# Layer 0's mixture of experts: the whole up product of the shared expert ahead of the first slot group

## The reference, cut to what matters

```
def _swiglu(x, wg, wu, wd):
    return jax.nn.silu(x @ wg) * (x @ wu) @ wd
logits = xn @ gate_w.T                      # xn: layernorm(x) * scale + bias
tk_probs, tk_idx = jax.lax.top_k(softmax(logits), 2)
w = ...                                     # the two weights of a token, made to sum to one
out = _swiglu(xf, sWg, sWu, sWd)            # the shared expert, all 512 tokens
for e in range(8):
    out = out + w[:, e:e + 1] * _swiglu(xf, Wg[e], Wu[e], Wd[e])
x = x + out
```

## Time and profile before

| | us |
|---|---|
| median of 3 runs | 3748.93 |
| lowest and highest run | 3747.81, 3753.61 |
| the profiled execution | 3748.13 |
| its span | 3746.2 |
| TensorE busy in the span | 3193.1 (85%) |
| mean DMA rate over the span | 175 GB/s |
| stage of the change | about 461 to 893 of the span |

### The profile page before, as it was taken

The page is one execution under the profiler, slowest core; times in us unless marked ns, Lnnn a source line. Parts: engine busy times, 40 slices in busy tenths (PEclk is TensorE's granted clock), DMA queues, the critical chain, the costliest instruction groups (busy, mean ns, idle before and its releaser), DMA issues. The chain is left out here.

```text
span 3746.2 us, 41895 instructions
## 1 busy us (share of the span) xinstructions
PE 3193.1 (85%) x16921; PEld 1560.7 (42%) x16921; DVE 1201.4 (32%) x2501; ACT 700.4 (19%) x1281; POOL 115.7 (3%) x148
## 2 busy tenths in 40 slices
PE   8998789985899799889688987798998897666666
PEld 4444443432444444344356564434444573111111
DVE  3555420002344579735232132212444411000000
ACT  2442101011233231100012120112343121000000
POOL 1000010001000000000000000000000100000000
PEclk9999889997899899979899999899998999787778
DMA  3100079995111212121440120692001236999998
GB/s 138 40 31 35 34 325 414 425 422 204 56 45 45 70 34 72 52 90 45 173 165 23 53 92 12 287 400 111 32 25 44 106 135 282 420 420 420 420 420 367
DMA packets 102709, 654.05 MB, mean 175 GB/s; under 512 B 18850, under 2 KB 28066, under 8 KB 39586
## 3 DMA queue, kind: packets, MB, share of 16 engines
q1 hardware_dynamic: 98402, 638.31, 42.2%
q0 software_dynamic: 4160, 13.63, 1.0%
HBM read 642.40 MB, written 9.50 MB: 174 GB/s over the span
## 5 line engine op out<-in xcount | busy, mean ns | idle before, releaser
L770 PE MATMUL banks<-wvb,ctxT 128*128 128x512 f32 x512 | 230.9, 596 | 0.0
L2654 PE MATMUL banks<-ring,h 128*32 128x512 f32 x1024 | 172.0, 791 | 65.6 <-DMA ring<-in_L_ffn_w 41.4
L2642 PE MATMUL banks<-ring,mine 128*32 128x512 f32 x1024 | 163.9, 703 | 71.3 <-DMA ring<-in_L_ffn_w 69.9
L1631 PE MATMUL banks<-ring,xT 128*64 128x512 f32 x736 | 165.5, 603 | 14.6 <-DMA ring<-in_L_ffn_Wu 6.8
L494 PE MATMUL banks<-normed_features,ctxT 128*128 128x256 f32 x768 | 168.0, 379 | 1.1 <-ACT normed_features L460 1.1
L494 PEld LDWEIGHTS banks<-normed_features,ctxT 128*128 128x128 f32 x768 | 144.6, 190 | 23.0 <-issue 3.2
L2743 DVE COPY mine<-mT 128x32 f32<-128x32 f32 x31 | 5.6, 181 | 449.6 <-PE banks L2642 449.6
L770 PEld LDWEIGHTS banks<-wvb,ctxT 128*128 128x128 f32 x512 | 92.8, 190 | 108.6 <-issue 106.2
L766 PE MATMUL banks<-extraT,wkb 128*128 128x512 f32 x256 | 116.9, 611 | 1.0 <-ACT extraT L876 1.0
L766 PE MATMUL banks<-ring 128*128 128x512 f32 x256 | 115.4, 595 | 1.4 <-PEq L141 1.4
L766 PE MATMUL banks<-ctxT,wkb 128*128 128x512 f32 x256 | 115.4, 595 | 1.4 <-PEq L141 1.4
(11 more groups left out here) (570 smaller groups left out, 4684.0 us busy)
## 6 DMA issues: line engine op xcount, KB each, us to landing
ring<-in_L_ffn_w SPq DMA_DIRECT2D x256, 1024.0 KB, 26.8
ring<-in_L_ffn_Wd SPq DMA_DIRECT2D x24, 2048.0 KB, 23.5
ring<-in_L_ffn_Wg SPq DMA_DIRECT2D x23, 2048.0 KB, 18.3
ring<-in_L_ffn_Wu SPq DMA_DIRECT2D x23, 2048.0 KB, 20.9
wa<-in_L_ffn_W SPq DMA_DIRECT2D x32, 1024.0 KB, 12.6
wb<-in_L_ffn_W SPq DMA_DIRECT2D x32, 1024.0 KB, 10.4
ctxT<-in_ctxT SPq DMA_DIRECT2D x16, 1024.0 KB, 4.9
extra<-in_ctx SPq DMA_DIRECT2D x8, 1024.0 KB, 6.8
```

The costliest lines, as they stand in the source:

```text
L770: ins = pe.matmul(ps[:, u % 2, :], ctxT[:, par, k, r * P:(r + 1) * P], wvb[:, k, :], start=(k == 0), stop=(k == C - 1))
L1631: ins = pe.matmul(ps[H * side:H * side + H, 2 * kind + half, :], xT[:, p % 2, k, H * own:H * own + H], rows_of(where[(name, slot)], C)[:, ...
L2642: ins = pe.matmul(ps[B4 * q:B4 * q + B4, 0, :], mine[:, e % 2, k, :], w[:, q * 512:(q + 1) * 512], start=(k == 0), stop=(k == C - 1))
L2654: ins = pe.matmul(ps[B4 * q:B4 * q + B4, 2, :], h[:, Q * n + q, :], w[:, q * D:(q + 1) * D], start=(n == 0), stop=(n == Q - 1))
```

## The change

The list of units starts with both up units, and none stands behind group 2. On TensorE, ScalarE and VectorE parts 4 to 7 of the shared up product follow parts 0 to 3, ahead of group 0; group 0 waits for all eight. The place behind group 2 and the wait ahead of group 3 are gone. No operation is added or dropped.

```
-    UP_AFTER, DOWN_AFTER = 2, 6
+    DOWN_AFTER = 6
...
-    units.append(("up", 0))
-    read_by.append((up_done, 4))
+    for half in range(2):
+        units.append(("up", half))
+        read_by.append((up_done, 4 * half + 4))
...
-        if p == UP_AFTER:
-            units.append(("up", 1))
-            read_by.append((up_done, FC))
...
-                for n in range(4):
+                for n in range(FC):
                     shared_up(n)
                     if n == 1:
                         rank()
-                pe.wait_ge(*hs_ready.at(4))
+                pe.wait_ge(*hs_ready.at(FC))
                 turn_x(0)
...
-                            if p == UP_AFTER + 1:
-                                pe.wait_ge(*hs_ready.at(FC))
...
-                    if p == UP_AFTER:
-                        for n in range(4, FC):
-                            shared_up(n)
...
-                for n in range(4):
+                for n in range(FC):
                     shared_silu(n)
-                act.wait_ge(*hs_ready.at(4))
+                act.wait_ge(*hs_ready.at(FC))
                 take_x(0)
...
-                    if p == UP_AFTER:
-                        for n in range(4, FC):
-                            shared_silu(n)
...
-                shared_h(3)
+                for n in range(3, FC):
+                    shared_h(n)
...
-                    if p == UP_AFTER:
-                        for n in range(4, FC):
-                            shared_h(n)
```

## The result

The changed kernel takes 3763.75 us (median of 9 runs, 3753.32 to 3772.1) against 3749.9 us for the kernel before (9 runs, 3745.13 to 3761.33). The ratio is 1.0030 with a 95% interval of 1.0018 to 1.0041, so +11 us, between +7 and +15. The two medians lie 13.9 us apart; the ratio is taken from the single runs. The forecast was +12 and 3761. The change is slower, and by about what was said; the scatter of whole executions is too wide to tell +10 from +12.

The account below looks back on a forecast made before the run. The prediction took the start of the unbroken weight stream and the units behind it to bound the stage. Its terms, 17.4 - 4.9 - 0.7 = +11.8 us, gave a median of 3761 us, range 3753 to 3768.

Parts of the forecast that it names:

- stream theory: Expert stage: the weight stream's start, set by group 0's first gate product, and the units behind it set the end; 74%.
- Step 1 and 2: Front of the stage: group 0 starts 19.4 us later, 2.08 us of clock come back, stream starts +17.4 us.
- Step 3: Ahead of the stream: a second unit gets through on idle engines, leaving 62 units instead of 63 behind; -4.9 us.
- Step 4: Behind group 2: without the block of parts 4 to 7 the queue no longer runs thin; -0.7 us, between 0 and 1.7.
- Step 5: Shared down product: frees nothing for 27.73 us, but seven of eight places in flight, 34 us, keep the queue fed; 0.
- Step 6: Other engines' passes, third load of rows and SyncE's extra 0.6 us issue long before the gate: all at nothing.
- TensorE as the bound: Rival for the stage: TensorE's chain sets the end, so the change gains -11.9 us, a median of 3737; 6%.
- The clock at the waits: Rival: TensorE's clock falls at waits for landings; in the last group up to 13 us more, 3774; 12%.
- each time: Skill's claim that waiting for a transfer between bursts always throttles the array again; by it the full 13 us are paid.

Follow-up runs that it names:

- e1: Kernel before with 32 additional matmuls, results unused, between part 3 and the first slot group; ratio to the kernel before 1.0049 (1.0031 to 1.0068).
- e5: Kernel before with the ranks computed behind part 0 instead of part 1, so the scatter of rows starts sooner; ratio 0.9974 (0.9963 to 0.9985).
- e2: Changed kernel with parts 4 to 7 cut to one of four contraction steps; ratio to the kernel before 0.9974 (0.9961 to 0.9986).
- e4: Kernel before with parts 4 to 7, behind group 2, cut to one of four contraction steps, all transfers kept; ratio 0.9995 (0.9982 to 1.0008).
- e11: Changed kernel, unedited, timed and profiled a second time; ratio to the kernel before 1.0022 (1.0013 to 1.0030).
- e7: Changed kernel with five units sent ahead and the other three issued at the start of the expert block; ratio to the kernel before 1.0020 (1.0010 to 1.0031).
- e3: Kernel before without the transfer of unit up 1; parts 4 to 7 read slot 5's Wd instead; ratio 0.9992 (0.9980 to 1.0004).
- e6: Kernel before with the unit issued at 515 held until the first slot group's rows have landed; ratio 0.9981 (0.9972 to 0.9990).
- e9: Kernel before with early ranks and the block of parts 4 to 7 with its unit behind group 3; ratio 0.9956 (0.9944 to 0.9969).
- e8: Kernel before with 8 additional unused matmuls in TensorE's wait ahead of the first rows' turn; ratio 1.0007 (0.9998 to 1.0017).
- e10: Kernel before without unit up 1's transfer and with parts 4 to 7 cut to one of four contraction steps; ratio 0.9970 (0.9960 to 0.9981).
- e12: Changed kernel with the ranks computed behind part 0; ratio to the kernel before 1.0031 (1.0020 to 1.0041).

## Why the prediction was right

The mechanism was right: the start of the stream and the transfers behind it set the end of the stage. The sizes of two terms were off, by -2.0 and +0.9 us, and the two misses partly cancel. That the time came within 1 us of the forecast is in part luck, since it scatters by more.

**The view that decided it** was the windows with their DMA share beside TensorE's near 85%. The stream theory's three statements hold: a late start goes through in full (e1), an early one too (e5), and work in the middle is worth little (e2, e4).

**Step 1 and 2, the start of the stream.** Forecast +17.4; measured +17.06 (e11) and +17.02 (e7); +21.03 in the one profile with the slow clock in front. The four parts took 27.5 to 27.7 us, the wait behind them 1.41, the turn 1.40, the clock came back.

**Step 3, the unit.** Forecast -4.9. From the stream's start to the last Wd product the queue of the ring moved 132.12 MB in the kernel before and 130.03 in the changed one, 63.0 and 62.0 units. B fell by 6.7 and 6.8 in both profiles of the changed kernel. e3 shows that the -4.9 is no property of the unit: it holds only because the block left the middle too.

**Step 4, the block,** was mis-sized: -0.7 forecast, from one dip less another. Summed over windows of 4 us from 600 to 672 against 427 GB/s, the kernel before loses 2.8 us, the changed one 0.2 and 0.1. So about -2.7. The prediction took the dip at 750 to 756 as the price of the slots' rows and subtracted it; but e4, with these rows and a short block, loses 0.2 us in the middle, so the dip behind the block was nearly all empty queue.

**Step 5 failed, by 1 us.** The down block was to cost nothing, with seven of eight places in flight for its 27.73 us. Over 720 to 792 the kernel before loses 1.1 us, the changed one 2.1 and 1.9. SyncE's queue and what q1 had moved, first in the kernel before (535.46 to 716.37, and to 865.38), then in the changed one (560.76 to 734.68, and to 883.96):

```profile
716.37 26.91 SPq L1520 DMA_DIRECT2D ring<-in_L_ffn_Wg  x2
749.97 1.44 SPq L1520 DMA_DIRECT2D ring<-in_L_ffn_Wu  x2
q1 hardware_dynamic: 5843, 71.91, 95.1%
q1 hardware_dynamic: 9984, 132.12, 95.3%
...
734.68 26.91 SPq L1518 DMA_DIRECT2D ring<-in_L_ffn_Wg  x2
768.27 1.44 SPq L1518 DMA_DIRECT2D ring<-in_L_ffn_Wu  x2
q1 hardware_dynamic: 4814, 70.22, 95.5%
q1 hardware_dynamic: 8928, 130.03, 95.3%
```

Both readings behind the zero were off. At 734.68 the changed kernel has 28.5 units still to move, 23 of them not yet issued, so 5.5 were in flight (5.7 in the kernel before), not seven: units that have landed keep their places until they are read. And the stretch to bridge is not the block but what lies between two freed pairs of places, 734.68 to 768.27 or 33.6 us, in which only the place of the shared Wd itself comes free. 6.5 units at 4.9 us last about 32 us (an estimate), and 0.2 units less in flight are about 1 us.

Why 0.2 units less is not settled by a run. TensorE being further ahead does not explain it: e6 and e9, with the block still in the middle, lose 2.2 and 3.0. What goes with the loss in all fourteen profiles is the clock in the last Wu or Wd product ahead of the down block. Here the changed kernel, then the kernel before:

```profile
715.12 8.78 PE L1627 MATMUL banks<-ring,xT 128*64 128x512 f32 x32 [4.00 <-DMA ring<-in_L_ffn_Wu]
...
697.07 7.09 PE L1631 MATMUL banks<-ring,xT 128*64 128x512 f32 x32 [1.22 <-DMA ring<-in_L_ffn_Wu]
...
707.45 7.09 PE L1654 MATMUL banks<-ring,hT 128*64 128x512 f32 x32 [1.78 <-DMA ring<-in_L_ffn_Wd]
```

The granted clock was 0.81 over 715 to 724 in the first, 1.00 in the second. Where both products took 7.09 us (the kernel before, e1, e4, e5, e8) the down block loses 0.7 to 1.3 us; where one took 8.78 to 9.44 (the other nine, both profiles of the changed kernel among them) it loses 1.9 to 3.0. A slower product ahead of the block lets more land before the next place comes free; this reading is argued, not tested.

In sum -4.9 - 2.7 + 0.9 = -6.7, which is what B shows. With A's +17.1 that is +10.4, against +11.8 forecast.

**Step 6** said that SyncE's extra issue was long before the gate. It was not always: 0.1 to 1.2 us.

**Rivals.** TensorE as the bound is excluded by e2, e4 and e5. TensorE lost its 9.4 us of idleness in front, and the kernel slowed; the general goal that the Trainium skill names ("Perfetto Trace Analysis", Optimizing DMA Performance) is not borne out in this stage. The clock at the waits did occur in the last group, in e2, e7 and e10 at a price of 1.6 to 1.7 us and in e4 at 0.5, not 13; in both profiles of the changed kernel the last Wd product was still set by its landing. There the falls came earlier and may be behind the 0.9 us of step 5. After waits of 3.3 us the product that followed took 7.09 in some groups and 8.8 to 10.0 in others, and in e11 after waits of 3.98 and 4.00 us it took 7.09 and 8.79, so "each time", as the Trainium skill has it for such waits ("TensorE: Matmul & The Clock Gate", HAM oscillation), does not hold here.

## What to carry to other kernels

Where weights stream through a ring, the end is set by when the stream starts without a break and by what follows it; work in front of the first freed place costs its full length beyond the idle time there, and taking it out of the middle gives back only what the queue had run dry there, and a transfer if one goes with it. Look for the stretch in which the DMA engines stand still with a full ring, and bring forward what frees its first place (here the ranks, 10 us for moving two calls). And a long block that frees nothing needs as many units in flight, not landed, as last from the place freed ahead of it to the next one freed behind it (here 33.6 us for a block of 27.7).

## What the runs showed that I had not expected

Times of whole executions of the same kernel spread over 20 us (3739.09 to 3763.17 for the kernel before beside e1 to e4), while A repeats within 0.4 us in the four kernels whose front is alike (74.01 to 74.35), and within 0.3 in e7, e11 and e12. The loss at the shared down product, a block that no edit touched, ran from 0.7 to 3.0 us, and it was high wherever the product just ahead of it had run at a fallen clock. Leaving out a transfer of 2 MiB from a stage bound by transfers made it no shorter (e3). A transfer of 256 KB issued just behind a 2 MiB unit lets its first waiting engine go 4.8 us later than when the unit is held back (9.37 against 4.55 us of waiting, e6).
